# Attention values for two heads at once, in units of token halves

## The chip, the cores and the metric

The kernel runs on one core of one Trainium2 chip. The metric is device time in microseconds (us), from the launch to the end of the execution, as the median of several runs. A core has five engines with instruction streams of their own: PE (TensorE, matrix products), ACT (ScalarE), DVE (VectorE), POOL (GpSimd) and SP (SyncE, which issues DMAs). They are ordered against each other only by semaphores.

## What is computed

A transformer block on x of shape (8, 512, 256): causal attention with 16 heads of queries and 4 groups of keys and values, then a mixture of 64 experts of which each token takes 6 (at most 64 tokens an expert and batch; a shared expert beside them).

```python
scores = jnp.einsum('bgqtd,bgksd->bgqts', q, k) / math.sqrt(D)   # D = 128, t = s = 512
scores = jnp.where(causal, scores, -jnp.inf)
probs = jax.nn.softmax(scores, axis=-1)
out = jnp.einsum('bgqts,bgksd->btgqd', probs, v).reshape(b, t, G * QPG * D)
return out @ wo
...
x = x + _layernorm(_L0_attn_ref(_layernorm(x)))
x = x + _layernorm(_L0_ffn_ref(_layernorm(x)))
```

## The kernel before

Every float32 number is split into a high and a low part of type float32r, and every product is three matmuls (high by high, high by low, low by high; `mm3`, whose matmuls stand at L661). The attention stage runs over N = 128 heads (8 batches of 16), `n` counts them, in a loop over `m` with one step per head. Each engine has this loop written out by hand with its own order of calls. Step `m` works on several heads at once: `scores(m, i)` for query block i = 3, 2, 1, 0 of 128 tokens against (i + 1) x 128 keys; `turn(m - 1, j)` and `turn(m - 2, 0)`, which transpose the probabilities of key block j (4 - j transpositions of 128x128 at L746); `values(m - 2, j)` for key blocks 3, 2, 1, 0, each a product of (4 - j) x 128 tokens into the one PSUM bank `bank_o`; and `project_out(m - 3)`, twelve matmuls of 256 columns into `bank_y0` and `bank_y1`, which gather the output of a batch over its 16 heads.

Between them stand the other engines. DVE adds the mask and takes each row's maximum (`maxima`, L1387, L1381), ACT takes the exponentials and row sums (L1035), DVE the inverses (L1394), POOL multiplies (`normalise`, L1811). After a turn ACT copies the high part out of PSUM into `pt_h` (`turned_high`, L1044) and DVE forms the low part `pt_l` (`turned_low`, L1400). After the last values of a head ACT makes `o_h` (`output_high`, L1051) and DVE `o_l` (`output_low`, L1406), each with one buffer; the next head's first values wait for `o_l`, since there is one `bank_o`. `pt` has one place for each key block.

Five PSUM banks (s0, t0, s1, t1, f) form a ring that the scores, the turned blocks and all other products take in turn; `RING_ORDER` says in which order, and a product waits until the fifth one before it has been taken out. The products of other stages are placed in the steps by the tables `BESIDE` (step within the batch, place in the step) and `QUIET`: the projections of queries (place 3 of every step), keys and values, the transposed input, and for the batch before it the router (`x2t`, `rt`, `mt`), the shared expert (`gu`, `sd`) and the layer norms (`stat1`, `norm1`, `stat2`, `norm2`). `picks(n)` places eight passes per batch in which DVE finds each expert's first 64 tokens (`pick`, L1477 and L1479); its table of steps is the same before and after.

After the loop come four drain steps, the last batch's router and shared expert, and the expert stage: SP streams 32 pairs of expert weights, POOL gathers tokens and scatters sums by indirect DMAs (L1947, L1960), and the end adds the sums. Eight weight pairs are loaded into the room of the attention weights; those past the first four and the next ones wait for `out_in` (the projections done) and `values_in`.

## Time and profile before

| | us |
|---|---|
| median of 3 runs (1413.05 to 1415.26) | 1414.33 |
| the profiled execution | 1414.98 |
| its span, first to last instruction | 1412.3 |
| PE busy in it | 1330.2 |
| DVE busy | 1098.3 |
| ACT busy | 843.9 |
| POOL busy | 801.3 |

All durations come from the one profiled execution. Its span is the time from the first to the last instruction; 2.7 us of the execution lie around it. Engines work beside each other, so the busy times do not add up. The attention stage reaches to about 1197 us, the drain included; the expert stage follows, and the final sums take the last 45 us or so.

### The profile page before, as it was taken

How to read it: one execution, taken by the hardware profiler on the slowest of the kernel's cores; microseconds unless marked ns; L12 is line 12 of the kernel's file. 1: busy time of each engine (PE TensorE's matmuls, PEld its weight loads, DVE VectorE, ACT ScalarE, POOL GpSimd, SP SyncE). 2: the span in 40 equal slices, each digit the busy share in tenths (PEclk: the TensorE clock that was granted, in tenths of full speed). 3: DMA queues.
4: the chain of work that ended last, by engine and by line, in shares of the span. 5: the costliest groups of instructions: out<-in, count | busy, mean ns of one | idle time of the engine just before them, and what ended most of it. 6: DMA issues, size and time to landing. Idle time of an engine off the chain costs nothing.

```text
span 1412.3 us, 27109 instructions
## 1 busy us (share of the span) xinstructions
PE 1330.2 (94%) x8987; PEld 1182.5 (84%) x8987; DVE 1098.3 (78%) x3652; ACT 843.9 (60%) x2322; POOL 801.3 (57%) x1054
## 2 busy tenths in 40 slices
PE   7999999999999999999999999999999999798950
PEld 5899999999999999999999999999999998754520
DVE  7777786889778977888788968897789788844438
ACT  6666665666666666666666656666666665543424
POOL 4666565556555655556555645565556554755644
PEclk9999999999999999999999999999999999999985
DMA  9100000100010001000100001000100016989986
GB/s 297 57 1 6 11 16 9 42 17 16 2 42 24 16 1 42 23 1 16 42 23 2 16 9 42 16 16 1 42 23 16 1 35 176 275 252 288 299 249 268
DMA packets 50507, 96.50 MB, mean 68 GB/s; under 512 B 4705, under 2 KB 36930, under 8 KB 50370
## 3 DMA queue, kind: packets, MB, share of 16 engines
q1 hardware_dynamic: 44226, 85.33, 18.8%
q0 software_dynamic: 6144, 9.44, 3.3%
q8 instruction: 74, 1.21, 0.4%
q14 instruction: 63, 0.52, 0.1%
HBM read 68.27 MB, written 26.49 MB: 67 GB/s over the span
## 4 chain that ended last, share of the span: by engine, by line
PE 84%; DVE 7%; DMA 3%; POOL 3%; issue 3%; ACT 1%; DVEq 0%; POOLq 0%
PE bank_s L661 18%; PE bank_t L661 17%; PE bank_o L661 17%; PE bank_y L661 13%; PE bank_f L661 8%; PE bank_t L746 4%; PE bank_s L746 4%; PE bank_f L746 2%; POOL ffn_sums L1960 2%; DMA ffn_sums<-dsum,idx_s 2%; POOL xg L1947 1%; DVE fstat L1743 1%; DVE fa L1738 1%; DVE first L1477 1%; DVE fa L1763 1%
## 5 line engine op out<-in xcount | busy, mean ns | idle before, releaser
L1811 POOL TENSOR_TENSOR prob<-prob,rinv 128x512 f32<-128x512 f32 (+3 forms) x512 | 368.6, 726 | 324.5 <-DVE rinv L1394 313.9
L1035 ACT ACTIVATE prob<-prob,negmax 128x512 f32<-128x512 f32 (+3 forms) x512 | 285.3, 557 | 83.0 <-DVE negmax L1381 77.0
L1798 POOL TENSOR_TENSOR q_l<-q_sum,q_h 128x128 fp32r<-128x128 f32 x254 | 182.4, 739 | 24.6 <-ACT q_h L1015 24.6
L661 PE MATMUL bank_o<-pt_h,v_h 128*128 128x128 f32 (+3 forms) x512 | 180.0, 352 | 0.5 <-DVE pt_l L1400 0.5
L661 PE MATMUL bank_o<-pt_l,v_h 128*128 128x128 f32 (+3 forms) x512 | 165.1, 323 | 0.0
L661 PE MATMUL bank_o<-pt_h,v_l 128*128 128x128 f32 (+3 forms) x512 | 165.1, 322 | 0.0
L661 PE MATMUL bank_y<-wo_h,o_h 128*128 128x256 f32 x512 | 143.7, 281 | 3.2 <-DVE o_l L1406 2.9
L661 PE MATMUL bank_y<-wo_h,o_l 128*128 128x256 f32 x512 | 143.6, 280 | 0.0
L661 PE MATMUL bank_y<-wo_l,o_h 128*128 128x256 f32 x512 | 143.0, 279 | 0.0
L1051 ACT ACTIVATE o_h<-bank_o,bkv_s 128x512 fp32r<-128x512 f32 x128 | 88.2, 689 | 78.4 <-PE bank_o L661 78.2
L1044 ACT ACTIVATE pt_h<-bank_t 128x512 fp32r<-128x512 f32 (+3 forms) x208 | 89.2, 429 | 53.0 <-PE bank_o L661 50.8
L1400 DVE TENSOR_TENSOR pt_l<-bank_t,pt_h 128x512 fp32r<-128x512 f32 (+3 forms) x208 | 100.6, 486 | 23.1 <-ACT pt_h L1044 22.4
L1044 ACT ACTIVATE pt_h<-bank_s 128x384 fp32r<-128x384 f32 (+3 forms) x198 | 84.5, 427 | 46.5 <-PE bank_o L661 43.4
L1400 DVE TENSOR_TENSOR pt_l<-bank_s,pt_h 128x384 fp32r<-128x384 f32 (+3 forms) x198 | 95.4, 484 | 19.6 <-ACT pt_h L1044 19.0
L661 PE MATMUL bank_s<-k_both,q_h 128*128 128x256 f32 (+2 forms) x362 | 104.8, 359 | 1.4 <-DVE wq_l L1294 1.4
L661 PEld LDWEIGHTS bank_y<-wo_h,o_h 128*128 128x128 f32 x512 | 96.2, 188 | 10.1 <-DVE o_l L1406 3.8
L661 PE MATMUL bank_t<-k_both,q_h 128*128 128x256 f32 (+2 forms) x352 | 100.7, 356 | 3.7 <-DVE negmax L1387 2.1
L661 PEld LDWEIGHTS bank_o<-pt_h,v_l 128*128 128x128 f32 x512 | 96.7, 189 | 5.6
L1387 DVE CUSTOM_DVE_ANT_0 prob<-bank_s,causal 128x512 f32<-128x512 f32 (+2 forms) x155 | 85.7, 553 | 20.0 <-PE bank_s L661 19.6
L661 PEld LDWEIGHTS bank_y<-wo_l,o_h 128*128 128x128 f32 x512 | 96.1, 188 | 5.4
L661 PEld LDWEIGHTS bank_o<-pt_h,v_h 128*128 128x128 f32 x512 | 96.7, 189 | 2.2 <-DVE pt_l L1400 2.1
L1035 ACT ACTIVATION_READ_ACCUMULATOR prob<-prob,negmax 128x1 f32 x512 | 97.8, 191 | 0.0
(456 smaller groups left out, 4113.9 us busy)
## 6 DMA issues: line engine op xcount, KB each, us to landing
w_gu<-in_w_in SPq DMA_DIRECT2D x32, 704.0 KB
w_dn<-in_w_out SPq DMA_DIRECT2D x32, 320.0 KB
xio<-in_x SPq DMA_DIRECT2D x16, 512.0 KB, 4.2
token_table<-rows SPq DMA_DIRECT2D x8, 640.0 KB, 3.7
ffn_sums<-keys SPq DMA_DIRECT2D x4, 1024.0 KB
x_rows<-xio SPq DMA_DIRECT2D x8, 512.0 KB, 3.0
ffn_sums<-ytr SPq DMA_DIRECT2D x16, 256.0 KB, 2.1
fx<-x_rows SPq DMA_DIRECT2D x8, 512.0 KB, 6.7
```

The source lines that it names most:

```text
L661: return pe.matmul(o, l, r, start=start, stop=stop, skip_group_check=True)
L746: last = pe.transpose(bk[:, (i - j) * P:(i - j + 1) * P], prob[:, r, tri[i] + j * P:tri[i] + (j + 1) * P], ident[:])
L1035: act.activation(p_, p_, ACT.Exp, bias=negmax[:, r, i:i + 1], scale=-1.0, accum_out=rsum[:, r, i:i + 1]).then_inc(exp_made, 1)
L1044: act.activation(pt_h[:, inv[j]:inv[j + 1]], bk[:, 0:(TT - j) * P], ACT.Copy).then_inc(pt_high, 1)
L1051: act.activation(o_h[:], bank["o"][:], ACT.Identity, bias=bkv_s[:, 2 * g + 1:2 * g + 2]).then_inc(o_high, 1)
L1387: dve.tensor_tensor_reduce(out=prob[:, r, tri[i]:tri[i + 1]], in0=bk[:, 0:w], in1=causal[:, T - w:T], scale=-1.0, scalar=BIG, op0=ALU.add, ...
L1400: dve.tensor_tensor(l_, bk[:, 0:(TT - j) * P], plain(h_), ALU.subtract).then_inc(taken, 1)
L1477: done(dve.max(o_, span))
L1738: dve.tensor_tensor(fa[b][:], fa[b][:], fb[b][:], ALU.add).then_inc(sum_dve, 1)
L1798: pool.tensor_tensor(l_[:, cols], sum_of(step)[:, cols], plain(h_)[:, cols], ALU.subtract).then_inc(pos_low, 1)
L1811: pool.tensor_tensor(p_, p_, rinv[:, r, i:i + 1].to_broadcast([P, (i + 1) * P]), ALU.mult).then_inc(prob_made, 1)
L1960: pool.indirect_dma_start(sums, bass.IndirectOffsetOnAxis(idx_s[:, j:j + 1].bitcast(U32), 0), dsum[j % ND][:], None, compute_op=ALU.add).t ...
```

## The change

- The values of two heads n and n + 1 of the same group are made at once, in two units: the later half of the tokens (key blocks 3, 2, 1, 0) and the earlier half (key blocks 1, 0). Units are counted by u, two for each pair; `bank_o`, `o_h` and `o_l` then hold 256 tokens of one head and 256 of the other. The later half comes first, but for the last pair, where the earlier does.
- `values(u, j)` runs at step u + 3 instead of n + 2, `project_out(u)` at step u + 4 instead of n + 3; a unit's projection goes into one bank, y1 or y0, for both heads.
- The turned blocks have 3, 3, 2 and 2 places for key blocks 0 to 3 instead of one each. The last place is for odd heads; even heads take the others in turn. `pt_pair` reads an even and an odd head's place as two runs.
- The steps come in two kinds, `even_step` and `odd_step`, on all engines, with `RING_ORDER` for each. The turn of key block 1 stays at the end of the step after its scores for odd heads; for even heads it goes to the start of the step after that. ACT waits before an odd unit's `output_high` for the projection before it.
- Room is made: keys have two places instead of four groups, the scratch of the shared expert's gates (`sig`, `gated`) lies in the second half of `ytr`, and the scratch for indirect DMAs is set to 8192 bytes. Seven entries of `BESIDE` and `QUIET` move: `v 1 1`, `x2t 0`, `rt 0`, `stat1`, `norm1`, `stat2` and `norm2`.
- DVE, ACT and POOL have the same calls as before in new orders of their own; of the diff's rest only renamed lookups are left out here.

```diff
-        k_both = place("k_both", [P, 2, NG, T], F32R)
+        k_both = place("k_both", [P, 2, 2, T], F32R)
...
-        inv = [P * (TT * j - j * (j - 1) // 2) for j in range(TT + 1)]
...
-        pt_h, pt_l = (place(f"pt_{s}", [P, tri[TT]], F32R) for s in "hl")
+        PLACES = (3, 3, 2, 2)
+        inv2 = [P * sum(PLACES[k] * (TT - k) for k in range(j)) for j in range(TT + 1)]
+        pt_h, pt_l = (place(f"pt_{s}", [P, inv2[TT]], F32R) for s in "hl")
...
-        sig = place("sig", [P, HT], F32)
-        gated = place("act", [P, HT], F32)
+        sig, gated = (ytr[:, 1, s * HT:(s + 1) * HT] for s in range(2))
...
         BESIDE = {
-            (0, 1): ("v", 0, 0), (1, 0): ("v", 0, 1), (3, 1): ("k", 1), (4, 2): ("v", 1, 0), (5, 2): ("x2t", 0),
-            (6, 1): ("rt", 0), (6, 2): ("v", 1, 1), (7, 1): ("k", 2), (7, 2): ("mt", 0), (8, 0): ("gu", 0, 0),
+            (0, 1): ("v", 0, 0), (1, 0): ("v", 0, 1), (3, 1): ("k", 1), (4, 2): ("v", 1, 0), (5, 2): ("v", 1, 1),
+            (6, 1): ("x2t", 0), (6, 2): ("rt", 0), (7, 1): ("k", 2), (7, 2): ("mt", 0), (8, 0): ("gu", 0, 0),
             (8, 1): ("gu", 0, 1), (8, 2): ("gu", 0, 2), (9, 0): ("sd", 0), (9, 1): ("x2t", 1), (9, 2): ("rt", 1),
             (10, 0): ("mt", 1), (10, 1): ("gu", 1, 0), (10, 2): ("gu", 1, 1), (11, 0): ("k", 3),
             (11, 2): ("gu", 1, 2), (13, 1): ("sd", 1), (14, 0): ("tx", 0), (14, 1): ("tx", 1), (15, 0): ("k", 0)}
 
         QUIET = {
-            (2, 3): ("stat1",), (3, 3): ("norm1",), (4, 1): ("stat2",), (5, 1): ("norm2",), (11, 0): ("statx",),
+            (3, 2): ("stat1",), (4, 1): ("norm1",), (5, 0): ("stat2",), (5, 3): ("norm2",), (11, 0): ("statx",),
             (13, 1): ("normx",)}
...
@@ -306,10 +309,41 @@
 
 
 
-        RING_ORDER = (("b", 3, 1), ("t", 0, 2), ("s", 3, 0), ("t", 3, 1), ("b", 0, 0), ("b", 1, 0), ("s", 2, 0),
-                      ("t", 2, 1), ("s", 1, 0), ("t", 1, 1), ("s", 0, 0), ("b", 2, 0))
-
-        V_ORDER, V_LATE = (3, 2, 1, 0), (2, 3)
+        RING_ORDER = (
+            (("b", 3, 1), ("t", 1, 2), ("t", 0, 2), ("s", 3, 0), ("t", 3, 1), ("b", 0, 0), ("b", 1, 0),
+             ("s", 2, 0), ("s", 1, 0), ("t", 2, 1), ("s", 0, 0), ("b", 2, 0), ("t", 1, 1)),
+            (("b", 3, 1), ("t", 0, 2), ("s", 3, 0), ("b", 0, 0), ("t", 3, 1), ("s", 2, 0), ("b", 1, 0),
+             ("t", 2, 1), ("s", 1, 0), ("s", 0, 0), ("b", 2, 0)))
+
+        UNIT_KEYS = ((1, 0), (3, 2, 1, 0))
+        PER_PAIR = sum(len(keys_) for keys_ in UNIT_KEYS)
+
...
+        def products(u, j):
+
+            p, before = u // 2, 0
+            if u % 2:
+                before = len(UNIT_KEYS[half_of(u - 1)])
+            return PER_PAIR * p + before + UNIT_KEYS[half_of(u)].index(j) + 1
...
+
+        def pt_of(t, n, j):
+
+            w = (TT - j) * P
+            k = PLACES[j] - 1 if n % 2 else first_place(n, j)
+            return t[:, inv2[j] + k * w:inv2[j] + (k + 1) * w]
+
+        def pt_pair(t, n, half, j):
+
+            lo, k = max(2 * half, j), first_place(n, j)
+            places_ = t[:, inv2[j]:inv2[j + 1]].rearrange("p (k t) -> p k t", k=PLACES[j])
+            return places_[:, k::PLACES[j] - 1 - k, (lo - j) * P:(2 * half + 2 - j) * P]
 
         def due(steps, n, ph):
...
-            return [slice(0, T)] if n < N - 1 else [slice(0, HT), slice(HT, T)]
+        TURNED = {}
+        for m in range(N + 4):
+            for n, j in (((m - 2, 1), (m - 2, 0), (m - 1, 3), (m - 1, 2), (m - 1, 1)) if m % 2 == 0 else
+                         ((m - 2, 0), (m - 1, 3), (m - 1, 2))):
+                if 0 <= n < N:
+                    TURNED[n, j] = len(TURNED) + 1
+
...
@@ -599,10 +646,10 @@
             sp.wait_ge(full, u + 1)
             for j in range(NWA):
                 if w_where[j] > wkv_end:
-                    sp.wait_ge(out_in, N + 1)
+                    sp.wait_ge(out_in, N)
                 load_pair(j)
-            sp.wait_ge(out_in, N + 1)
-            sp.wait_ge(values_in, 4 * N)
+            sp.wait_ge(out_in, N)
+            sp.wait_ge(values_in, PER_PAIR * N // 2)
...
-            def values(n, j):
+            def values(u, j):
+                n = u // 2 * 2
                 b, h = divmod(n, NQ)
-                g = h // QPG
-
-                _, _, low, u = use("t", n, j)
-                pe.wait_ge(low, u + 1)
-                if j == V_ORDER[0] and h % (2 * QPG) == 0:
-                    _, _, taken, u = use("v", b, g // 2, 1)
-                    pe.wait_ge(taken, u + 1)
-                    _, _, taken, u = use("v", b, g // 2, 0)
-                    pe.wait_ge(taken, u + 1)
-                if j == V_ORDER[0] and n:
-                    pe.wait_ge(o_low, n)
-                mm3(bank["o"][:, j * P:T], [v[:, j, g * P:(g + 1) * P] for v in (v_h, v_l)],
-                    [q[:, inv[j]:inv[j + 1]] for q in (pt_h, pt_l)], start=j == V_ORDER[0]).then_inc(values_in, 1)
-
-            def project_out(n):
+                g, half = h // QPG, half_of(u)
+
+                for r in range(2):
+                    _, _, low, use_ = use("t", n + r, j)
+                    pe.wait_ge(low, use_ + 1)
+                if j == UNIT_KEYS[half][0]:
+                    if not u % 2 and h % (2 * QPG) == 0:
+                        for s2 in range(2):
+                            _, _, taken, use_ = use("v", b, g // 2, s2)
+                            pe.wait_ge(taken, use_ + 1)
+                    if u:
+                        pe.wait_ge(o_low, u)
+                o_ = bank["o"][:].rearrange("p (r t) -> p r t", r=2)
+                mm3(o_[:, :, (max(2 * half, j) - 2 * half) * P:], [v[:, j, g * P:(g + 1) * P] for v in (v_h, v_l)],
+                    [pt_pair(q, n, half, j) for q in (pt_h, pt_l)], start=j == UNIT_KEYS[half][0]).then_inc(values_in, 1)
+
+            def project_out(u):
+                n, half = u // 2 * 2, half_of(u)
                 b, h = divmod(n, NQ)
-                pe.wait_ge(o_low, n + 1)
+                pe.wait_ge(o_low, u + 1)
                 if h == 0 and b:
-                    pe.wait_ge(y0_out, b)
-                    pe.wait_ge(y1_out, b)
-
-                for i in range(TT):
-                    if n == N - 1 and i == TT // 2:
-
-                        last.then_inc(out_in, 1)
+                    pe.wait_ge((y0_out, y1_out)[half], b)
+
+                for r in range(2):
+                    if u == N - 1 and r:
                         pe.wait_ge(o_low, N + 1)
-                    last = mm3(bank[f"y{i // 2}"][:, i % 2 * E:(i % 2 + 1) * E],
-                               [o_[:, i * P:(i + 1) * P] for o_ in (o_h, o_l)], [w[:, h, :] for w in (wo_h, wo_l)],
-                               start=h == 0 and i % 2 == 0)
+                    for i in range(2):
+                        at_ = slice(r * HT + i * P, r * HT + (i + 1) * P)
+                        last = mm3(bank[f"y{half}"][:, i * E:(i + 1) * E], [o_[:, at_] for o_ in (o_h, o_l)],
+                                   [w[:, h + r, :] for w in (wo_h, wo_l)], start=h == r == i == 0)
                 last.then_inc(out_in, 1)
...
-            for m in range(N + 4):
+            def even_step(m):
+                beside(m - 1, 3)
+                if has(m - 2):
+                    turn(m - 2, 1)
+                    turn(m - 2, 0)
+                if has(m):
+                    scores(m, 3)
+                if has(m - 3):
+                    for j in UNIT_KEYS[half_of(m - 3)][0:2]:
+                        values(m - 3, j)
+                if has(m - 3):
+                    for j in UNIT_KEYS[half_of(m - 3)][2:]:
+                        values(m - 3, j)
+                if has(m - 1):
+                    turn(m - 1, 3)
+                beside(m, 0)
+                beside(m, 1)
+                if has(m - 4):
+                    project_out(m - 4)
+                if has(m):
+                    scores(m, 2)
+                    scores(m, 1)
+                if has(m - 1):
+                    turn(m - 1, 2)
+                if has(m):
+                    scores(m, 0)
+                beside(m, 2)
+                if has(m - 1):
+                    turn(m - 1, 1)
+
+            def odd_step(m):
                 beside(m - 1, 3)
                 if has(m - 2):
                     turn(m - 2, 0)
                 if has(m):
                     scores(m, 3)
-                if m == 3:
-                    pe.wait_ge(*low_made(4))
+                if has(m - 4):
+                    project_out(m - 4)
+                beside(m, 0)
                 if has(m - 3):
-                    project_out(m - 3)
+                    for j in UNIT_KEYS[half_of(m - 3)][0:1]:
+                        values(m - 3, j)
                 if has(m - 1):
                     turn(m - 1, 3)
-                if has(m - 2):
-                    values(m - 2, 3)
-                beside(m, 0)
+                if has(m):
+                    scores(m, 2)
                 beside(m, 1)
-                if has(m):
-                    scores(m, 2)
                 if has(m - 1):
                     turn(m - 1, 2)
-                if has(m - 2):
-                    values(m - 2, 2)
-                if has(m - 2):
-                    values(m - 2, 1)
-                if has(m - 2):
-                    values(m - 2, 0)
                 if has(m):
                     scores(m, 1)
-                if has(m - 1):
-                    turn(m - 1, 1)
+                if has(m - 3):
+                    for j in UNIT_KEYS[half_of(m - 3)][1:]:
+                        values(m - 3, j)
                 if has(m):
                     scores(m, 0)
                 beside(m, 2)
+
+            for m in range(0, N + 4, 2):
+                if m == 4:
+                    pe.wait_ge(*low_made(4))
+                even_step(m)
+                odd_step(m + 1)
...
-                if n and j in V_LATE:
-                    act.wait_ge(values_in, 4 * n - 3 + V_ORDER.index(j))
+                if n > 1 and n % 2 == 0 and j >= 2:
+                    act.wait_ge(values_in, products(n - 2, j))
+                if n > 3 and n % 2 == 0 and j < 2:
+                    act.wait_ge(values_in, products(n - 3, j))
+                if n > 1 and n % 2 and j < 2:
+                    act.wait_ge(values_in, products(n - 2, j))
                 act.wait_ge(full, u + 1)
-                act.activation(pt_h[:, inv[j]:inv[j + 1]], bk[:, 0:(TT - j) * P], ACT.Copy
-                               ).then_inc(pt_high, 1)
-
-            def output_high(n):
-                g = n % NQ // QPG
-
-                act.wait_ge(values_in, 4 * n + 4)
+                act.activation(pt_of(pt_h, n, j), bk[:, 0:(TT - j) * P], ACT.Copy).then_inc(pt_high, 1)
+
+            def output_high(u):
+                g = u // 2 * 2 % NQ // QPG
+
+                if u % 2:
+                    act.wait_ge(out_in, u)
+                act.wait_ge(values_in, products(u, UNIT_KEYS[half_of(u)][-1]))
                 act.activation(o_h[:], bank["o"][:], ACT.Identity, bias=bkv_s[:, 2 * g + 1:2 * g + 2]
                                ).then_inc(o_high, 1)
 
...
+                if 0 < b < L1 and k == n == 0:
+
+                    act.wait_ge(dma_ffn[1], 16 * b)
...
+    nc = bacc.Bacc("TRN2", target_bir_lowering=False, num_devices=1,
+                    dynamic_dma_scratch_size=8192)
...
```

## Rows read from the trace of the kernel before

**Rows 1.** The page, part 1: busy us (share) xinstructions of each engine.

```profile
PE 1330.2 (94%) x8987; PEld 1182.5 (84%) x8987; DVE 1098.3 (78%) x3652; ACT 843.9 (60%) x2322; POOL 801.3 (57%) x1054
```

**Rows 2.** Busy time by stretch, columns: us, engines' busy, PEclk, DMA share, GB/s.

```profile
...
340.00:490.00 150.00, 150.00 (x1035) 138.84 (x1033) 124.63 (x418) 93.90 (x260) 84.55 (x118) 1.00 0.06 20
...
```

**Rows 3.** Waits of PE, 40 to 1180 us: total, times, longest, all in us.

```profile
PE bank_o L661 <- DVE pt_l L1400: 0.5, 1, 0.5
PE bank_y L661 <- POOL wo_l L1865: 0.4, 1, 0.4
```

**Rows 4.** Timeline of PE: start us, us, engine, line, operation, out<-in, shape, count.

```profile
508.31 0.38 PE L746 MATMUL bank_f<-ident,prob 128*128 128x128 f32 x2
508.44 0.36 PE L661 MATMUL bank_o<-pt_h,v_h 128*128 128x256 f32 x1
...
508.88 0.34 PE L661 MATMUL bank_o<-pt_h,v_h 128*128 128x384 f32 x1
...
509.40 0.39 PE L661 MATMUL bank_o<-pt_h,v_h 128*128 128x512 f32 x1
...
510.10 0.39 PE L661 MATMUL bank_s<-k_both,q_h 128*128 128x256 f32 x2
...
510.69 0.36 PE L661 MATMUL bank_s<-k_both,q_h 128*128 128x256 f32 x1
510.89 0.22 PE L661 MATMUL bank_s<-k_both,q_l 128*128 128x128 f32 x1
...
513.81 0.60 PE L746 MATMUL bank_s<-ident,prob 128*128 128x128 f32 x4
514.16 0.71 PE L661 MATMUL bank_t<-k_both,q_h 128*128 128x512 f32 x2
514.71 0.39 PE L661 MATMUL bank_t<-k_both,q_l 128*128 128x512 f32 x1
514.94 0.28 PE L661 MATMUL bank_y<-wo_h,o_h 128*128 128x256 f32 x1
...
516.35 0.27 PE L746 MATMUL bank_s<-ident,prob 128*128 128x128 f32 x1
516.37 0.31 PE L661 MATMUL bank_o<-pt_h,v_h 128*128 128x128 f32 x1
...
516.74 0.45 PE L661 MATMUL bank_t<-xn_h,wkv_h 128*128 128x512 f32 x1
```

**Rows 5.** Busy time by stretch, single steps of the fourth batch, then all.

```profile
470.78:478.41 7.63, 7.63 (x52) 7.03 (x51) 7.36 (x23) 4.89 (x13) 3.94 (x6) 1.00 0.01 3
567.86:575.48 7.62, 7.62 (x52) 7.02 (x51) 7.02 (x23) 5.25 (x16) 4.74 (x7) 1.00 0.00 0
585.22:593.68 8.46, 8.46 (x60) 7.85 (x59) 8.05 (x25) 5.99 (x17) 4.30 (x7) 1.00 0.22 62
452.71:602.68 149.97, 149.97 (x1034) 138.79 (x1032) 124.60 (x417) 93.88 (x260) 84.54 (x118) 1.00 0.06 20
```

**Rows 6.** Groups by line and shape: count, busy us, mean ns, idle before.

```profile
L1406 DVE SCALAR_TENSOR_TENSOR o_l<-bank_o,bkv_s,o_h 128x512 fp32r<-128x512 f32 x127 | 95.1, 749 | 0.0
L1051 ACT ACTIVATE o_h<-bank_o,bkv_s 128x512 fp32r<-128x512 f32 x128 | 88.2, 689 | 78.4 <-PE bank_o L661 78.2
L1477 DVE MAX8 first<-keys 64x8 f32<-64x576 f32 x64 | 47.6, 745 | 0.3
```

**Rows 7.** Timeline of PE and DVE at both ends of the attention stage.

```profile
31.15 0.50 PE L661 MATMUL bank_t<-k_both,q_h 128*128 128x256 f32 x2 [2.15 <-DVE negmax L1387]
...
1183.14 0.36 PE L661 MATMUL bank_t<-k_both,q_h 128*128 128x256 f32 x1
...
1195.10 0.39 PE L661 MATMUL bank_y<-wo_h,o_h 128*128 128x256 f32 x1 [1.37 <-DVE o_l L1406]
1195.35 0.74 DVE L1477 MAX8 first<-keys 64x8 f32<-64x576 f32 x1
```

**Rows 8.** Waits of GpSimd (POOL) in the expert stage, 1225 to 1370 us.

```profile
POOL ffn_sums L1960 <- DMA ffn_sums<-dsum,idx_s: 33.8, 22, 3.7
```

301 lines of the change are left out of this document (202 added, 99 removed).

## The prediction

> **What bounds the kernel now.** I read four views, in this order. First the page's line of busy shares [rows 1]: PE (TensorE) is at 94%, DVE (VectorE) at 78%, so PE is the first suspect. Second, the busy time of every engine in a stretch of 150 us out of the attention stage [rows 2]: PE is busy for 150.00 of 150.00 us at the full clock (granted share 1.00, which is the 2.4 GHz level), with DVE at 83% and the DMA engines at 0.06. Third, what PE waited for between 40 and 1180 us [rows 3]: 0.9 us in all. So some 1140 of 1412 us are paced by PE alone: whatever PE issues less there comes straight off the span, as long as no other engine becomes late. Fourth, the starts of PE's instructions within a step (a step is one head of one batch; there are 128) [rows 4]. A row's duration there is no price, since matmuls overlap; the price of one is the distance from its start to the next start.
>
> **Prices on PE** [rows 4]. A matmul of 512 columns is issued every 0.233 us (509.40 to 510.10 holds three), of 384 every 0.173 (508.88 to 509.40 holds three), of 256 every 0.118 (the twelve of an output projection take 1.41, from 514.94 to 516.35). One of 128 columns costs 0.11: from 516.37 to 516.74 there are three in 0.37, of which 0.03 to 0.04 is the late start behind a transposition. So 128 columns cost nearly what 256 do. A group of transpositions costs about 0.11 each: four take 0.35 and the matmul after them starts 0.09 late (two of 512 columns take 0.55, not 0.466); two take 0.13 and the next group of 256 is 0.085 long (508.44 to 508.88 is 0.44, not 0.354). A single one before a 128-column matmul is cheap: 0.02 plus 0.04.
>
> **Part 1, values for two heads at once.** Before, one head has twelve value matmuls: three each of 128, 256, 384 and 512 columns: 0.33 + 0.354 + 0.52 + 0.70 = 1.90 us, so 3.81 for two heads. After, two heads are two units (the later and the earlier half of the tokens). The later half has key blocks 3, 2, 1, 0 with 256, 512, 512, 512 columns, the earlier has 1, 0 with 256, 512; three matmuls each. That is 6 of 256 and 12 of 512: 0.71 + 2.80 = 3.50. The columns are the same 7680; gone are six matmuls that cost 0.11 for 128 columns. Gain 0.31 per pair, all of it on the path, since PE waits for nothing: 64 x 0.31 = 20 us.
>
> **Part 2, the order of the turned blocks.** There are 10 transpositions per head as before. The cheap pairing (one transposition, then a 128-column matmul: 0.06) is gone, since that matmul is gone; the single one now stands before longer matmuls, at 0.11. So transpositions go from 1.05 to 1.10 per head: +0.05, times 128 = +6.4 us. Net on PE 20 - 6.4 = 13.6 by the rounded prices; with 0.1115 and 0.1755 for 128 and 384 columns, which more rows of the same kind average, 14.4, which I take.
>
> **Part 3, reads and writes in two runs.** The pairs read the turned blocks as two runs. A read in two runs is in the trace: the 256-column score matmul at 510.69 reads the keys' high and low parts so, and its 0.20 to the next start is that of the 256-column group behind transpositions too (0.085 late) [rows 4]. I take no cost. A write in two runs (blocks 3 and 1, 256 columns, two groups per pair) has no row; between nothing and the largest irregularity that the rows show, 0.085 per group, that is 0 to 2 x 0.085 x 64 = 11 us. I take 0, since the two-run read costs nothing; a gain is excluded, as the columns remain.
>
> **Part 4, other engines.** ACT (ScalarE) and DVE copy and subtract as many blocks as before: 128 output extractions at 0.69 and 0.75 us [rows 6], all turned blocks, all score reductions. DVE's work per plain step stays at 7.0 us with a pick (8 of 16 steps; its two passes are 0.745 each [rows 6]), so at 5.5 without. The function that says which steps pick is not touched and the trace already holds all 64 first picks, so picks cost nothing more. PE's steps become uneven: an even step has 3 + 3 value matmuls (1.05 us) and 13 transpositions, an odd one 2.45 us and 7. A plain step of 7.62 us becomes about 7.1 (even) and 7.9 (odd). DVE's margin is thinnest in even steps with a pick: 7.02 of 7.62 now (the step from 567.86) [rows 5], then 7.0 of 7.1; the step from 585.22 has 8.05 of 8.46, and 0.48 less is below DVE's work. Each is followed by an odd step that gives 0.25 back. The statistics move: the first from the third step of a batch, which would be short, to the fourth, where it meets a key projection, a pick and the copy of y; there DVE has about 10.3 us of work against 9.3 of PE, and in the sixth 9.8 against 9.3. DVE then runs some 1.5 to 2 us behind. Now it runs as far behind after the step from 470.78, where it has statistics and a pick and is busy for 7.36 of 7.63, and PE does not wait [rows 3, 5].
>
> **New waits.** (a) The values of an even step start with a wait for the extraction of the unit that ended the odd step. Behind it in PE's order stand everything else of the step and so DVE's and ACT's next reads. Cover: from the end of the values to that point PE has scores of block 0 (0.26), the query projection (six of 512, 1.40), 4 + 3 transpositions (0.77) and the scores of block 3 (0.70): 3.1 us against 0.69 + 0.75 = 1.44. Hidden unless DVE is 1.7 us later than now. Without that cover it costs up to 1.44 per pair. (b) The single output buffer: ACT's extraction of an odd unit waits for the projection of the unit before; the projection of 1.41 comes right after the values in the same step, and 3 us of other PE work follow. Queued behind it on ACT are block 3 to 0 exponentials, whose results PE needs a step later. Hidden. (c) ACT holds block 2's copy in an odd step until values 2 are done, now 0.58 us later (scores of block 1 stand between); ACT is busy for 5 to 6.7 us of a step [rows 5]. Hidden, with (a) if ACT is late. (d) The key tiles have two places instead of four: the place written was read last four steps before. (e) The gate's scratch now shares the block that SyncE stores: the store is some ten steps old. No queue is moved past. I allow 1.5 us in all for lateness out of (a) to (c), between 0 and the price of the second rival.
>
> **Part 5, both ends.** The pipeline is one step deeper. At the start PE waits 2.15, 0.49 and 0.40 us in steps that also split weights [rows 3, 7]; step 2 loses the values that filled it (about +0.9), the wait for the output weights gets one step more (-0.4): +0.5. At the end, the last two units are serial: extraction of the last but one, values of the last (2.45), extraction, projection. Worked through with 0.69 and 0.75 per extraction, the time from the last score matmuls (1183.14) to the end of the last projection (1195.10 + 1.41 = 1196.5) [rows 7] grows from 13.4 to about 17.2, of which 2.5 is work counted in part 1 and only moved: +1.3. Against that, the last pick (from 1195.35, 0.74 and a copy) now holds up the statistics of the first half of y, whose projection is done 0.7 after 1195.10 [rows 7]; then it lies under the last values, and one half of y is ready a projection earlier: -0.5. Net +0.8.
>
> **Part 6, the smaller scratch for indirect DMAs.** GpSimd's scatters already wait 33.8 us for earlier scatters to land and at most seven gathers run ahead [rows 8]. I take 0; bounds -1 to +3 us.
>
> **The sum.** The profiled run took 1414.98 us with a span of 1412.3, 0.65 above the median of 1414.33. -14.4 + 1.5 + 0.5 + 0.8 = -11.6. 1414.98 - 11.6 = 1403.4, and against the median 1402.7.
>
> **Rivals.**
> 1. DVE becomes the pace where it picks. For: 7.02 of 7.62 and 8.05 of 8.46 [rows 5]. Against: it follows PE within a step and odd steps give back. Half of the 14.4 lost: 1402.7 + 7.2 = 1409.9. Chance 0.15.
> 2. Slower: wait (a) is exposed. Place: first value matmul of each even step. DVE must be 1.7 us later than now there; PE's gain is gone when the mean stall is 0.18 + 0.02 us per pair. If it stalls 0.7 us in five of eight pairs (those with picks or statistics), 64 x 0.44 = 28, less the 1.5 allowed: 1429. Against: DVE's lag of that size costs PE nothing now. Chance 0.10.
> 3. Writes in two runs cost 0.085 per group: 1402.7 + 11 = 1413.6. Chance 0.06.
> 4. A matmul costs its columns alone (0.055 for 128), so the 20 us of part 1 are nearly zero, and the costs of the other parts stay: 1422.7. The rows speak against it (0.11 for 128 columns, not 0.055). Chance 0.02.
> The Trainium skill, "TensorE: Matmul & The Clock Gate", Back-to-back issue gap, gives N/2.4 + 2.5 ns for an isolated warm matmul, 56 ns at 128 columns, and by that rival 4 would be right. The trace disagrees, with 111 ns here.
>
> **How the numbers follow.** Forecast 0.66, its own range 1398 to 1407 (scratch and lateness each way). Rest of chance 0.01 unexplained. Range 1397 to 1413: it takes in rival 1 and nearly rival 3, and leaves out rivals 2 and 4. A measurement tells apart about 0.2%, 2.8 us. Faster by more (below 1411.5): forecast and rival 1, 0.80; within: rival 3 and edges, 0.08; slower: 0.12.
>
> **What would show it.** PE still 150 of 150 us busy in mid-attention; a batch of 16 steps takes 148.2 us instead of 149.97 (the last row) [rows 5]; value matmuls 6 and 12 per pair at 0.118 and 0.233; even plain steps near 7.1, odd near 7.9. Wrong if PE waits appear at bank_o for o_l or pt_l, if 256-column value matmuls are spaced wider than 0.13, or if the stretch from the last projection to the end is not near 215.8 us.

## The result, and the profile after

The changed kernel takes 1392.47 us (median of 4 runs, 1390.69 to 1393.81), the kernel before 1413.69 beside it (1412.5 to 1415.26): a ratio of 0.9848, with a 95% interval of 0.9831 to 0.9866. The spans of the profiled executions are 1412.3 and 1390.1 us. The direction is as forecast, and 21.2 us came off where 11.6 were forecast; 1392.47 lies below the forecast's range (1397 to 1413).

First the busy time by stretch of the changed kernel (columns as in [rows 2]): the 150 us of [rows 2], two plain even steps with a pick, the whole fourth batch.

```profile
340.00:490.00 150.00, 150.00 (x1005) 136.79 (x1004) 128.68 (x432) 97.47 (x266) 85.83 (x122) 1.00 0.06 20
459.73:466.45 6.72, 6.72 (x47) 6.10 (x46) 6.65 (x22) 5.11 (x15) 3.08 (x5) 1.00 0.01 2
554.63:561.35 6.72, 6.72 (x47) 6.10 (x46) 6.65 (x22) 5.11 (x15) 3.78 (x7) 1.00 0.00 0
...
442.05:588.75 146.70, 146.70 (x986) 133.88 (x985) 126.04 (x417) 95.30 (x260) 83.46 (x117) 1.00 0.06 20
```

PE is still busy for all of the 150 us, so it is still the bound, at the same granted clock of 1.00. The batch took 149.97 us [rows 5] and takes 146.70: 3.27 us less, 0.41 per pair of heads, where 0.225 was forecast. DVE is now busy for 6.65 of 6.72 us in an even step with a pick: 0.07 us from being the bound there.

What PE waited for in 40 to 1180 us (columns as in [rows 3]):

```profile
PE bank_o L708 <- DVE o_l L1526: 2.4, 2, 1.7
PE bank_y L708 <- DVE o_l L1526: 1.9, 2, 1.4
PE bank_s L794 <- DVE pt_l L1520: 0.4, 1, 0.4
```

The four waits of the first two lines all lie behind 1158 us, in the drain; the last is at 40.6. From there to the drain PE waits for nothing.

The starts of PE's instructions in the plain even step from 554.63, and the odd step's values (columns as in [rows 4]):

```profile
554.86 0.28 PE L708 MATMUL bank_o<-pt_h,v_h 128*128 128x256 f32 x1
554.98 0.28 PE L708 MATMUL bank_o<-pt_l,v_h 128*128 128x256 f32 x1
555.10 0.28 PE L708 MATMUL bank_o<-pt_h,v_l 128*128 128x256 f32 x1
555.22 0.40 PE L708 MATMUL bank_o<-pt_h,v_h 128*128 128x512 f32 x1
555.45 0.40 PE L708 MATMUL bank_o<-pt_l,v_h 128*128 128x512 f32 x1
555.68 0.39 PE L708 MATMUL bank_o<-pt_h,v_l 128*128 128x512 f32 x1
555.92 0.27 PE L794 MATMUL bank_s<-ident,prob 128*128 128x128 f32 x1
555.94 0.36 PE L708 MATMUL bank_y<-wo_h,o_h 128*128 128x256 f32 x1
556.14 0.28 PE L708 MATMUL bank_y<-wo_l,o_h 128*128 128x256 f32 x1
...
557.42 0.51 PE L708 MATMUL bank_t<-k_both,q_h 128*128 128x384 f32 x2
...
557.95 0.41 PE L708 MATMUL bank_s<-k_both,q_h 128*128 128x256 f32 x2
...
566.67 0.40 PE L708 MATMUL bank_o<-pt_h,v_h 128*128 128x512 f32 x1
...
568.73 0.28 PE L708 MATMUL bank_f<-k_both,q_h 128*128 128x256 f32 x1
```

The 256-column values that write in two runs are 0.12 apart, as those of an output projection are. Nine of 512 columns in a row take 568.73 - 566.67 = 2.06: 0.228 each, not 0.233. The twelve matmuls of an output projection take 1.48 here, behind one transposition, where they took 1.41 behind score matmuls [rows 4]: the first is 0.20 from the second, not 0.12.

The drain of the changed kernel, PE alone (the wait in front in brackets):

```profile
1158.63 0.35 PE L708 MATMUL bank_o<-pt_h,v_h 128*128 128x256 f32 x1 [0.69 <-DVE o_l L1526]
...
1162.99 0.38 PE L708 MATMUL bank_y<-wo_h,o_h 128*128 128x256 f32 x1 [0.58 <-DVE o_l L1526]
...
1167.45 0.36 PE L708 MATMUL bank_o<-pt_h,v_h 128*128 128x256 f32 x1 [1.73 <-DVE o_l L1526]
...
1172.88 0.38 PE L708 MATMUL bank_y<-wo_h,o_h 128*128 128x256 f32 x1 [1.36 <-DVE o_l L1526]
```

The last scores (of query block 0) start at 1156.82 and the last projection ends at 1174.38: 17.56 us, where it was 13.47 (1183.14 to 1196.61) [rows 7]. From there to the end of the span it is 215.7 us in both kernels. So all of the gain is made between step 3 and the last step (1133.7 us before, 1107.9 after: -25.9); the drain takes 4.1 of it back, and the start changes by 0.7.

### The profile page after: what moved, and what is told of

The parts are those of the page before. It is cut to its first block, busy times and chain, and to the rows that moved or that the text cites. A ratio compares the mean times of both kernels' runs of the same rounds, so it can differ in the third digit from the quotient of the medians.

```text
span 1390.1 us, 26790 instructions
## 1 busy us (share of the span) xinstructions
PE 1304.2 (94%) x8603; PEld 1142.8 (82%) x8603; DVE 1109.6 (80%) x3652; ACT 855.3 (62%) x2322; POOL 793.7 (57%) x1054
## 3 DMA queue, kind: packets, MB, share of 16 engines
q0 software_dynamic: 6144, 9.44, 3.3%
## 4 chain that ended last, share of the span: by engine, by line
PE 84%; DVE 5%; POOL 4%; DMA 3%; issue 3%; ACT 1%; POOLq 0%; DVEq 0%
PE bank_t L708 18%; PE bank_s L708 17%; PE bank_o L708 16%; PE bank_y L708 13%; PE bank_f L708 8%; PE bank_t L794 4%; PE bank_s L794 4%; POOL ffn_sums L2144 2%; PE bank_f L794 2%; DMA ffn_sums<-dsum,idx_s 2%; POOL xg L2131 1%; DVE fstat L1905 1%; DVE fa L1900 1%; DVE fa L1925 1%; DMA xg<-token_table,idx_g 0%
## 5 line engine op out<-in xcount | busy, mean ns | idle before, releaser
L1973 POOL TENSOR_TENSOR prob<-prob,rinv 128x512 f32<-128x512 f32 (+3 forms) x512 | 362.0, 725 | 250.9 <-DVE rinv L1514 250.5
L1127 ACT ACTIVATE pt_h<-bank_t 128x256 fp32r<-128x256 f32 (+3 forms) x208 | 89.8, 432 | 80.5 <-PE bank_t L794 73.1
L708 PE MATMUL bank_o<-pt_h,v_h 128*128 128x512 f32 (+1 forms) x384 | 136.6, 356 | 2.4 <-DVE o_l L1526 2.4
L1127 ACT ACTIVATE pt_h<-bank_s 128x512 fp32r<-128x512 f32 (+3 forms) x203 | 88.2, 434 | 79.4 <-PE bank_s L794 74.2
L708 PE MATMUL bank_o<-pt_l,v_h 128*128 128x512 f32 (+1 forms) x384 | 136.7, 356 | 0.0
L708 PE MATMUL bank_o<-pt_h,v_l 128*128 128x512 f32 (+1 forms) x384 | 136.0, 354 | 0.0
L1135 ACT ACTIVATE o_h<-bank_o,bkv_s 128x512 fp32r<-128x512 f32 x128 | 87.8, 686 | 44.9 <-PE bank_y L708 26.3
L1520 DVE TENSOR_TENSOR pt_l<-bank_t,pt_h 128x256 fp32r<-128x256 f32 (+3 forms) x208 | 99.7, 481 | 8.5 <-ACT pt_h L1127 6.9
L1520 DVE TENSOR_TENSOR pt_l<-bank_s,pt_h 128x512 fp32r<-128x512 f32 (+3 forms) x203 | 97.9, 484 | 7.8 <-ACT pt_h L1127 6.3
L1526 DVE SCALAR_TENSOR_TENSOR o_l<-bank_o,bkv_s,o_h 128x512 fp32r<-128x512 f32 x129 | 95.9, 744 | 7.0 <-ACT o_h L1135 7.0
L1507 DVE CUSTOM_DVE_ANT_0 prob<-bank_t,causal 128x256 f32<-128x256 f32 (+2 forms) x147 | 80.8, 549 | 19.6 <-PE bank_t L708 19.1
```

Source lines behind the costliest of these rows:

```text
L708: return pe.matmul(o, l, r, start=start, stop=stop, skip_group_check=True)
L1127: act.activation(pt_of(pt_h, n, j), bk[:, 0:(TT - j) * P], ACT.Copy).then_inc(pt_high, 1)
L1135: act.activation(o_h[:], bank["o"][:], ACT.Identity, bias=bkv_s[:, 2 * g + 1:2 * g + 2]).then_inc(o_high, 1)
L1507: dve.tensor_tensor_reduce(out=prob[:, r, tri[i]:tri[i + 1]], in0=bk[:, 0:w], in1=causal[:, T - w:T], scale=-1.0, scalar=BIG, op0=ALU.add, ...
L1520: dve.tensor_tensor(l_, bk[:, 0:(TT - j) * P], plain(h_), ALU.subtract).then_inc(taken, 1)
L1526: dve.scalar_tensor_tensor(out=o_l[:, cols], in0=bank["o"][:, cols], scalar=bkv_s[:, 2 * g + 1:2 * g + 2], in1=plain(o_h[:, cols]), op0=AL ...
```

## Where the 0.41 us per pair come from

A segment is a run of PE instructions of one kind, and its price the distance from its first start to the first start of the next kind. Added up over the plain steps of both kernels (of odd steps after the change, which all have a product placed beside, without that product), per pair, in us. "Late" is how much later than its usual spacing the next group starts, and stands in the row of what precedes it.

| per pair | before | after | change | forecast |
|---|---|---|---|---|
| value matmuls by their spacing | 3.82 | 3.47 | -0.35 | -0.325 |
| transpositions, with the late start behind them | 2.10 | 2.19 | +0.09 | +0.10 |
| late start of the score group behind three 128-column values | 0.12 | 0 | -0.12 | not seen |
| all other groups | 9.20 | 9.17 | -0.03 | 0 |
| sum | 15.24 | 14.83 | -0.41 | -0.225 |

(The single-step sum of plain steps is 15.24 before and 6.71 + 8.11 = 14.82 after.)

By the recorded starts of the matmuls the third row is the miss. It can be read in the kernel before, in the step of [rows 5] that starts at 567.86:

```profile
569.51 0.27 PE L746 MATMUL bank_s<-ident,prob 128*128 128x128 f32 x1
569.53 0.31 PE L661 MATMUL bank_o<-pt_h,v_h 128*128 128x128 f32 x1
569.68 0.27 PE L661 MATMUL bank_o<-pt_l,v_h 128*128 128x128 f32 x1
569.79 0.28 PE L661 MATMUL bank_o<-pt_h,v_l 128*128 128x128 f32 x1
569.90 0.57 PE L661 MATMUL bank_t<-k_both,q_h 128*128 128x384 f32 x2
570.31 0.34 PE L661 MATMUL bank_t<-k_both,q_l 128*128 128x384 f32 x1
570.48 0.38 PE L746 MATMUL bank_s<-ident,prob 128*128 128x128 f32 x2
```

Three 384-column scores take 0.58 (569.90 to 570.48) behind the 128-column values, and 0.53 (557.42 to 557.95) in the changed kernel, where a projection stands before them. The place that the prediction read its 128-column price from (516.37 to 516.74, [rows 4]) is followed by another kind of group, and it took the distance inside the group alone. A narrow group leaves its successor 0.055 us late, as a transposition does.

The weight loads show what this lateness is. Every matmul and every transposition has a weight load of its own, PEld in the profile, nearly all of them 128x128. The loads at the same place of the kernel before (columns as in [rows 4]):

```profile
569.40 0.14 PEld L746 LDWEIGHTS bank_s<-ident,prob 128*128 128x128 f32 x1
569.51 0.19 PEld L661 LDWEIGHTS bank_o<-pt_h,v_h 128*128 128x128 f32 x1
569.62 0.19 PEld L661 LDWEIGHTS bank_o<-pt_l,v_h 128*128 128x128 f32 x1
569.73 0.19 PEld L661 LDWEIGHTS bank_o<-pt_h,v_l 128*128 128x128 f32 x1
569.84 0.30 PEld L661 LDWEIGHTS bank_t<-k_both,q_h 128*128 128x128 f32 x2
```

From 569.51 on they start 0.11 us apart, and so does the next one behind them (569.95, the second of the last row). Between 60 and 1150 us 99% of all loads in this kernel start at least 0.10 us after the one before, however few columns are multiplied between. Among wide matmuls each load starts together with the matmul before its own. Among narrow ones the loads are further apart than the columns take, and a matmul is recorded as starting 0.02 to 0.06 after the start of its own load (569.53 and 569.51, 569.90 and 569.84), where it is 0.12 among 256-column matmuls (569.15 and 569.27 in the projection just before). What looks cheap at the head of such a group (0.02 + 0.04 for the single transposition) comes back as the late start behind it. From load to load the single transposition and the three matmuls are four times 0.11 us. In the router's product at 506.78 to 507.67 matmuls of 128 and 64 columns alternate: their recorded starts are 0.14 and 0.08 apart in turn, their loads 0.11 every time.

So the same 0.41 us can be counted from load to load, which leaves no late starts over: a matmul's price is then the distance between the two loads that follow its own. In the fourth batch a transposition is 0.109 us before and 0.110 after, all transpositions together 2.46 and 2.47 us per pair; the value matmuls are 3.85 and 3.46 (0.110, 0.120, 0.179 and 0.233 for 128, 256, 384 and 512 columns before; 0.118 and 0.230 for 256 and 512 after); the rest is 0.03 less. By this count rows two and three of the table belong together, and the forecast's +0.10 for the transpositions is what did not come.

## Experiments

The kernel before, run beside the first four of these, took 1414.41 us; beside the doubled pick, the changed kernel again and the first run of the drain 1414.24; beside the other two 1415.08.

### Do the columns cost, or the matmuls? Block 3 widened to 256

In the kernel before. The block-3 values read a part of the output weights in place of the turned block, since that is 256 columns wide, so the attention result is not the reference's.

```diff
+                if j == V_ORDER[0]:
+                    mm3(bank["o"][:, 2 * P:T], [v[:, j, g * P:(g + 1) * P] for v in (v_h, v_l)],
+                        [w[:, 0, :] for w in (wo_h, wo_l)], start=True).then_inc(values_in, 1)
+                    return
```

> Kernel before, with key block 3's three value matmuls made 256 columns wide instead of 128 (they read output weights in place of probabilities, so attention's result is not the reference's; counts and waits as before, and one wait for the first output weights at step 2). Theory A (a group of 128-column matmuls costs more than its own 0.366 us: the group after it starts 0.055 us late, since 0.581 was taken by three 384-column matmuls that take 0.527 elsewhere): 0.354 + 0.085 (late behind the transposition) for 0.366 + 0.055, so +0.02 us per head, +2 us: 1416. Theory B (the prices as forecast, no late start behind narrow matmuls): +0.07 per head, +9 us: 1423. Columns alone: +0.16 per head, +20 us: 1434.

Measured: 1416.83 us (1415.25 to 1420.19), ratio 1.002 (1.0002 to 1.0039). Theory A holds, and theory B and columns alone are refuted. From step 3 to the last step it is 3.0 us more, 0.024 per head (A: 0.02, B: 0.07). The same place of the same step (columns as above):

```profile
571.28 0.27 PE L746 MATMUL bank_s<-ident,prob 128*128 128x128 f32 x1
571.31 0.36 PE L661 MATMUL bank_o<-wo_h,v_h 128*128 128x256 f32 x1
571.51 0.28 PE L661 MATMUL bank_o<-wo_l,v_h 128*128 128x256 f32 x1
571.63 0.28 PE L661 MATMUL bank_o<-wo_h,v_l 128*128 128x256 f32 x1
571.75 0.52 PE L661 MATMUL bank_t<-k_both,q_h 128*128 128x384 f32 x2
572.10 0.34 PE L661 MATMUL bank_t<-k_both,q_l 128*128 128x384 f32 x1
572.28 0.38 PE L746 MATMUL bank_s<-ident,prob 128*128 128x128 f32 x2
```

From the single transposition to the next pair it is 1.00 us, against 0.97 before. The values themselves take 0.44 (0.37 before), and the scores behind them 0.53 (0.58 before): twice the columns for 0.03 us. B's +0.07 came from the 0.06 that the forecast put for a single transposition before a 128-column matmul: it took that cheap pairing to be lost here, and the run shows that there was none to lose.

### Block 3 left out

In the kernel before, without the block-3 value matmuls and the counts that go with them; the last key block's share of the last 128 tokens is left out.

```diff
-        V_ORDER, V_LATE = (3, 2, 1, 0), (2, 3)
+        V_ORDER, V_LATE = (2, 1, 0), (2,)
...
-                if has(m - 2):
-                    values(m - 2, 3)
```

> Kernel before without key block 3's three value matmuls (128 columns) in every head; the last 128 tokens do not see their last key block, all else is as before, but for ACT's copy of block 3, which waits for no values. Theory A: per head 0.366 + 0.055 go, and the single transposition now makes the scores behind it 0.085 - 0.03 late: -0.33 to -0.36 us per head, -43 to -46 us: 1369. Theory B (prices as forecast): -0.28 us, -36 us: 1378. If DVE becomes the pace (7.0 us of work in a plain step with a pick against 7.3 of PE): less than either in those steps.

Measured: 1382.26 us (1376.94 to 1383.27), ratio 0.9749 (0.9722 to 0.9777). The total lies nearer B's number (1378) than A's (1369), a plain step by A's. A plain step, the whole batch, and its fifth step:

```profile
551.90:559.20 7.30, 7.30 (x49) 6.67 (x48) 7.04 (x23) 5.27 (x16) 4.74 (x7) 1.00 0.00 0
439.79:585.41 145.62, 145.22 (x985) 133.44 (x984) 124.00 (x417) 93.43 (x261) 84.52 (x118) 1.00 0.06 20
473.16:483.00 9.84, 9.44 (x61) 8.07 (x60) 9.10 (x35) 5.65 (x17) 8.51 (x11) 1.00 0.15 55
```

A plain step falls from 7.62 to 7.30, by 0.32 to 0.33 us (A: 0.33 to 0.36; B, the forecast's own prices, 0.28). But the fifth step takes 9.84 us, 0.47 more than in the kernel before (9.37) where 0.33 less was due. PE stands in it for 0.40 us (9.44 of 9.84), for turned blocks that DVE had not yet subtracted; the two steps before it carry statistics and picks. These 0.80 us, once a batch, are most of what the total lacks. They suggest what the change avoided by moving the statistics: in the order of before, part of a gain can be given back in this step.

### The changed kernel with each value matmul split by head

The layout, the order and the steps of the changed kernel, with the matmuls of half the width: 128 columns where it has 256, 256 where it has 512.

```diff
-                mm3(o_[:, :, (max(2 * half, j) - 2 * half) * P:], [v[:, j, g * P:(g + 1) * P] for v in (v_h, v_l)],
-                    [pt_pair(q, n, half, j) for q in (pt_h, pt_l)], start=j == UNIT_KEYS[half][0]).then_inc(values_in, 1)
+                for r in range(2):
+                    last = mm3(o_[:, r, (max(2 * half, j) - 2 * half) * P:],
+                               [v[:, j, g * P:(g + 1) * P] for v in (v_h, v_l)],
+                               [pt_pair(q, n, half, j)[:, r, :] for q in (pt_h, pt_l)],
+                               start=j == UNIT_KEYS[half][0] and not r)
+                last.then_inc(values_in, 1)
```

> Kernel after in all its order, waits and places, but with each value matmul made once per head (128 or 256 columns) instead of once for the two. Per pair 12 matmuls of 128 for 6 of 256 and 24 of 256 for 12 of 512. Theory A (the gain is in the widths, and narrow groups make the next late): +0.63 + 0.06 + 2 x 0.055 = +0.8 us per pair, +50 us over after: 1442, slower than before. Theory B (widths as forecast, no late start): +0.68, +42 us: 1435. Theory C (the gain beyond the forecast is in the new order of the steps, not in the widths): below before, under 1413.

Measured: 1434.83 us (1432.38 to 1441.16), ratio 1.0147 (1.0113 to 1.0181). Theory C (that the gain is of the order, not of the width) is refuted: without the width the kernel is slower than before. A batch is 152.55 us, 5.85 more than in the changed kernel, 0.73 per pair: between B's 0.68 and A's 0.80, nearer B's. The total meets B's number, partly by chance: from step 3 to the last step it is 44.9 us more than in the changed kernel, and the stretch behind the last projection, which the edit doesn't touch, was 5.6 us shorter in this profile (210.1 against 215.7). A counted the late starts on top of the 0.11 per matmul, and the rows show why that was too much:

```profile
575.20 0.22 PE L708 MATMUL bank_o<-pt_h,v_h 128*128 128x128 f32 x1
575.25 0.28 PE L708 MATMUL bank_o<-pt_l,v_h 128*128 128x128 f32 x1
575.37 0.27 PE L708 MATMUL bank_o<-pt_h,v_l 128*128 128x128 f32 x1
...
575.70 0.28 PE L708 MATMUL bank_o<-pt_h,v_l 128*128 128x128 f32 x1
575.81 0.33 PE L708 MATMUL bank_o<-pt_h,v_h 128*128 128x256 f32 x1
575.98 0.28 PE L708 MATMUL bank_o<-pt_l,v_h 128*128 128x256 f32 x1
```

Here 0.11 to 0.12 lie between them again, but the first and second are only 0.05 apart, so the six recorded distances add up to 0.62; and the first of the 256-column group has 0.17 to its next, not 0.12: 0.05 late once more. The two belong together, and six matmuls of 128 columns cost 0.67 with both, 0.11 each. The late start is no cost beside that.

### Only the 512-column matmuls split

The same edit, but the groups of 256 columns stay as they are (the branch cut short here).

```diff
+                if j > 2 * half:
...
+                    return
+                for r in range(2):
+                    last = mm3(o_[:, r, :], [v[:, j, g * P:(g + 1) * P] for v in (v_h, v_l)],
+                               [pt_pair(q, n, half, j)[:, r, :] for q in (pt_h, pt_l)], start=False)
+                last.then_inc(values_in, 1)
```

> Kernel after, with only the 512-column value matmuls made once per head (24 of 256 columns for 12 of 512 per pair); the narrow blocks (256 columns) stay paired. Theory A: 24 x 0.118 for 12 x 0.2305 = +0.07 us per pair, +4 us: 1397, so nearly all of the gain is in pairing the narrow blocks. A theory in which wide matmuls carry the gain (0.85 as many columns per us at 256): +0.2 us per pair or more, 1405 and up.

Measured: 1398.45 us (1395.21 to 1401.74), ratio 0.9877 (0.9848 to 0.9905). A's number was 1397, and the theory that 512 columns as such are the gain (1405 or more) is refuted by the time. A batch is 147.83 us, +1.13, 0.14 per pair, where A said 0.07 and the other 0.2 or more; eighteen of 256 columns take 2.155 where nine of 512 take 2.056. So of the 0.73 us per pair that splitting both widths undoes, 0.14 is for 512 against 256 and the rest, 0.59, for 256 against 128.

### How near the bound DVE is: the pick's first pass done twice

The same line doubled in both kernels, which adds 0.75 us of DVE work to each of the 64 picks.

```diff
                 done(dve.max(o_, span))
+                done(dve.max(o_, span))
```

> Kernel before, with the first of the two passes of a pick done twice, in all batches but the last (same result): +0.76 us of DVE work in 56 of 128 steps, 43 us in all. PE's margin over DVE in plain pick steps is 7.62 against 6.84 + 0.76 = 7.60: just hidden; the step with statistics and the one after, where DVE already lags by 2.6 us, then reach 4 us or more and PE waits: +1 to +2 us per batch, +7 to +14 us. If DVE has room throughout: +0. If DVE were the pace: +43.

> Kernel after with the same extra pass. Over the eight pick steps of a batch PE takes 68.0 us and DVE's busy time is 61.9; with 6.1 more it is 68.0, so the margin is used up: if DVE can run behind and catch up within these steps, +0 to +2 us per batch (+0 to +14 us); if every even step stalls by its own lack (6.64 + 0.76 - 6.71 = 0.7, four of them a batch): +2.8 per batch, +20 us. If DVE were already the pace in after (my first rival): +43.

Measured: before 1427.39 us (1425.39 to 1432.15), ratio 1.0086 (1.0066 to 1.0106), +13; changed 1412.85 us (1409.31 to 1416.4), ratio 0.999 (0.9976 to 1.0005), 19 over the unedited changed kernel beside it (1393.94). That is far from the +43 of a kernel whose pace DVE sets. The step from 558.64 and its place of waiting in the changed kernel so edited:

```profile
558.64:565.92 7.28, 7.12 (x47) 6.18 (x45) 7.18 (x23) 5.16 (x15) 3.60 (x7) 1.00 0.00 0
```

```profile
563.04 0.55 PE L794 MATMUL bank_s<-ident,prob 128*128 128x128 f32 x3 [0.16 <-DVE pt_l L1520]
```

DVE's 0.75 us make this step 0.57 longer (6.71 before the edit), and the odd step behind it not at all. By steps of a batch the cost is 0.57 + 0.34 + 0.57 + 0.79 (the third, fifth, thirteenth and fifteenth), 2.2 us, and the other picks are free; from step 3 to the last it is 14.2 us. In the kernel before so edited the plain step is not longer (7.63 with 7.53 of DVE work); only the third to fifth are, and it is 7.0 us to the last step. Another 6.3 us of both are the last batch's eight picks, which stand one behind the other after the attention stage: 8 x 0.79. No expectation had counted that part, so the totals came near the numbers of +14 and +20 partly by it: what the steps show is 7.0 and 14.2.

### The drain: a bank of its own for the last unit

The changed kernel, with the last unit's values in a bank of the ring that is free by then, in place of bank_o, so that they don't wait for the extraction of the unit before.

```diff
+        def bank_of(u):
+            return use("t", N - 1, OWN)[0] if u == N - 1 else bank["o"]
...
-                    if u:
+                    if 0 < u < N - 1:
                         pe.wait_ge(o_low, u)
-                o_ = bank["o"][:].rearrange("p (r t) -> p r t", r=2)
+                o_ = bank_of(u)[:].rearrange("p (r t) -> p r t", r=2)
```

> Kernel after, unchanged, beside the others of this job: 1392, ratio to before 0.985.

> Kernel after, but the very last unit's values go into a ring bank that is free by then, instead of waiting 1.73 us for the one output bank to be emptied of the unit before. Theory A (the deeper pipeline costs its serial end: values, extraction, values, extraction, projection): the extraction of the last but one unit now lies beside the last values; the last projection starts 1.7 us earlier: -1.7 us to after. Rival (the end is set by DVE's picks or by ACT's single output buffer anyway): no difference.

> The changed kernel with the last unit's values in a bank of their own, once more, for two questions that the first run left. One: its drain was 2.0 us shorter, but step 1 at the start, which the edit doesn't touch, was 10.74 us instead of 12.78 in its profile. If that is chance of one execution, this profile has 11.8 to 12.8 us there and the last projection ends at 1172.4 (1174.4 less 2.0); if it goes with the kernel, it has 10.7 again and the last projection ends at 1170.9. Two: from the last projection's end to the end the first run took 218.0 us where the changed kernel takes 215.7 to 216; if that is chance it is 215.5 to 216.5 here. Time by the first theory in both: 1390 to 1391.5; by the second in both: 1389.5 to 1390.5.

Measured: the changed kernel again 1393.94 us (1392.66 to 1396.45), ratio 0.986 (0.984 to 0.9881); with the edit 1389.69 (1387.6 to 1390.82), ratio 0.9819 (0.9801 to 0.9837), and, run again, 1388.34 (1387.59 to 1390.74), ratio 0.981 (0.9787 to 0.9833). So this version beats both kernels; against the changed one the two ratios beside each other, 0.9819 and 0.986, differ by 0.4%. PE's waits in the drain of the second run:

```profile
1157.80 0.35 PE L713 MATMUL bank_o<-pt_h,v_h 128*128 128x256 f32 x1 [0.69 <-DVE o_l L1531]
1162.16 0.39 PE L713 MATMUL bank_y<-wo_h,o_h 128*128 128x256 f32 x1 [0.58 <-DVE o_l L1531]
1170.09 0.38 PE L713 MATMUL bank_y<-wo_h,o_h 128*128 128x256 f32 x1 [1.37 <-DVE o_l L1531]
```

The wait of 1.73 is gone and the others stay; from the last scores to the end of the last projection it is 15.6 us, 2.0 less. The median moved by 4.3 us. Of the two questions of the second run: step 1 took 12.09 us there, between the 12.78 and 10.74 of before, and the stretch to the end 214.6 us against 217.9 in the first. So both vary from one execution to the next by 1 to 3 us, whatever the edit; the 2.0 us of the drain are shown by the rows, the rest of the median's move is not assigned.

### The smaller scratch for indirect DMAs

In the kernel before, that edit alone.

```diff
-    nc = bacc.Bacc("TRN2", target_bir_lowering=False, num_devices=1)
+    nc = bacc.Bacc("TRN2", target_bir_lowering=False, num_devices=1,
+                    dynamic_dma_scratch_size=8192)
```

> The kernel before with one edit: the scratch for the descriptors of indirect DMAs is 8192, as in the changed kernel. Theory A (part 6 of the prediction): the scatters of the expert stage already wait for earlier scatters to land (33.8 us in 22 waits in the kernel before) and the gathers run at most seven ahead, so nothing changes: 1414.2 +- 1.5 us, and the time from the last projection's end to the end of the span stays at 215.7 us. Theory B: GpSimd has to wait for room in the smaller scratch: +1 to +3 us, seen as a longer time from the last projection to the end and as longer or more waits of the gathers (11.4 us in 30 or 31 waits on no visible releaser so far). A gain would mean that the room itself cost time somewhere; neither theory has it.

Measured: 1413.31 us (1411.65 to 1418.43, 12 runs), ratio 0.9989 (0.9975 to 1.0003). No cost can be told: the interval leaves at most 0.4 us upwards. GpSimd's own rows in this kernel, 1190 us to the end:

```profile
POOL ffn_sums L1960 <- DMA ffn_sums<-dsum,idx_s: 30.6, 18, 4.1
...
POOL xg L1947 <- issue: 11.2, 28, 3.0
```

Neither kind of wait has grown (33.8 in 22 [rows 8], and 11.1 in 28 in the kernel before). The stretch behind the last projection was 217.7 us in its profile, within what that stretch varies by.

## Why the prediction was right in sign and short in size

- **What bounds the kernel.** Right. PE was busy for 150.00 of 150.00 us before and after, so every 0.01 us per pair of PE time was 0.64 us of the span.
- **Part 1, the values.** Right in mechanism, and a little short: from load to load -0.385 us per pair where -0.325 was forecast, 3.8 us in all. The 0.11 for 128 columns holds. Of the difference 0.036 is that 512-column matmuls cost 0.230 in the changed kernel, where up to nine stand in a row, and 0.233 before; 0.02 is that the 384-column ones cost 0.179 and not 0.1755. Splitting the values of the changed kernel costs 0.73 us per pair.
- **Part 2, the transpositions.** This is the step that failed. It took the single transposition in front of a 128-column matmul for a cheap pairing (0.06) that the change loses, and charged 0.05 us per head, 6.4 us in all. From load to load every transposition costs 0.11 us before and after, and the change is +0.01 per pair, not +0.10: 6.0 us of the miss. By recorded starts the same error reads as the table has it: the late start behind the single transposition (+0.09) was counted as new, while the late start behind the narrow group that it replaced (-0.12) was not counted as gone. Widening block 3 in the kernel before, where the same pairing is lost, costs 0.024 us per head and not the 0.07 of the forecast's prices.
- **Part 3, two runs.** Right: 0. The 256-column values that write two runs are 0.118 apart, and nine 512-column pairs that read and write two take no longer than any others. Rival 3 (1413.6) is refuted by these rows.
- **Part 4, DVE.** Right in kind. Even steps with a pick fit by 0.07 us. The forecast put 7.1 and 7.9 for even and odd steps; cut between the same score matmuls they are 6.71 and 8.11, but that cut puts seven transpositions of the even step into the odd one and four of the odd into the even; cut at the query projections, as the program has them, they are about 7.0 and 7.8. The fourth step, for which 10.3 us of DVE work were forecast, has DVE busy for 9.24, and PE does not wait there, as forecast. Rival 1 (1409.9) is refuted for this kernel; the doubled pick shows that its mechanism was named rightly, and that the stall is 0.34 to 0.79 us in four steps of a batch where a pick is 0.75 us longer.
- **The new waits.** (a) to (e) cost nothing outside the drain: 1.5 us had been allowed, 0 was found. Rival 2 (1429) is refuted: no wait of PE on bank_o before 1158 us.
- **Part 5, the ends.** Drain: 17.2 forecast, 17.56 measured; the stretch behind it 215.8 forecast, 215.7 measured. The start came out 0.7 better, not 0.5 worse. Net of the pairs' own gain (64 x 0.41 = 26.2 against 22.2 on the span) the ends cost 4.0 us, where 2.8 were forecast for them and lateness. The drain's 2.5 us of "moved" values stand in that: the work that leaves the start was not wholly won there.
- **Part 6, the scratch.** Right: 0.
- **Rival 4, columns alone.** Refuted twice: doubling the columns of block 3 costs 0.03 us per head (columns alone say 0.16), and halving all widths costs 0.73 us per pair. The rule of the Trainium skill ("TensorE: Matmul & The Clock Gate", Back-to-back issue gap) for an isolated matmul, a gap of N/2.4 + 2.5 ns, 56 ns at 128 columns, doesn't hold in these rows, which have 110 to 112 ns; at 512 columns it gives 216 ns and the rows 228 to 233. The same section says that in a stream of weight loads and matmuls both set the spacing. There the trace agrees, but the figures given for such a stream, about 81 ns at 128 columns and 131 ns at 512, are not those of these rows either.

By these terms the forecast of -11.6 becomes -11.6 - 6.0 (part 2) - 3.8 (part 1) - 2.0 (the other groups' 0.03 per pair) + 1.2 (the ends) = -22.2, which is what the spans differ by. The 2.0 for the other groups have no cause found.

The range was too narrow because it took in unknown costs on one side only. "A gain is excluded" was right for the two-run writes, but no bound was set on the 0.06 of the cheap pairing, read at one place where the next group's late start was not looked at. With anything from that 0.06 to the 0.11 of all other transpositions, the range would have reached 6.4 us lower, to 1390.6, and taken in 1392.47. The weight loads, busy for 138.84 of 150 us [rows 2], were not looked at either.

## What to carry to other kernels

Where every matmul has its own weight load, price narrow matmuls and transpositions by the starts of the loads, here never much under 0.11 us apart. If matmul starts are used, a group's price ends only where the group after it has fallen into its usual spacing: a short distance at the head of a narrow group comes back as a late start behind it. Where PE is busy all the time, merging two matmuls of 128 columns into one of 256 is worth nearly a whole matmul, and of two of 256 into one of 512 almost nothing (here 0.59 us for twelve narrow ones turned into six, 0.14 us for twenty-four turned into twelve). After such a change look at the engine that comes next: here VectorE has 0.07 us left in its fullest steps, so a further saving on TensorE may not be won there; that was not tried.
